# Additions of attention probabilities split by columns between VectorE and GpSimd, and ternary transposes at other steps

## The chip, the cores and the metric

The kernel runs on one core of a Trainium2 chip. The metric is the device time of one execution in microseconds. The engines in the tables: PE is TensorE (PEld its weight loads), DVE is VectorE, ACT is ScalarE, POOL is GpSimd, and SP issues nearly all DMAs.

## The reference

One transformer layer in float32: differential attention and a feed-forward layer with ternary weights, each behind a layer norm and with a residual. Shapes: 8 batches, 1024 rows, 512 columns, 16 heads of 32, hidden width 2048.

```python
qkv = x @ w_qkv                      # q, k split in halves of 16 columns per head: q1, q2, k1, k2
a1 = softmax(q1 @ k1.T * scale)
a2 = softmax(q2 @ k2.T * scale)
lam = exp(dot(lambda_q1, lambda_k1)) - exp(dot(lambda_q2, lambda_k2)) + 0.8
out = (a1 - lam * a2) @ v
out_n = out / rms(out) * norm_w * 0.2
x = x + rearranged(out_n) @ wo
# feed-forward
h = x @ (tern(w_fc) * scale).T + gate * (x @ v.T @ fast_b.T @ u.T)
x = x + relu(h) ** 2 @ (tern(w_proj) * scale).T
```

`tern(w)` is w over its row's mean magnitude, rounded and clipped to -1, 0, 1. What the change touches is the denominator of the softmax and the preparation of the ternary weights.

## The kernel before

The first phase (to about 130 us) loads and splits weights and projects the first batch. Then comes a loop over 64 pairs of heads, P = 0 to 63, eight for each batch (NP = 8). A pair has 16 steps, k = 0 to 15: j = k // 8 chooses the first or second softmax, t = k % 8 one of eight blocks of 128 key rows. The code counts in eight double steps d, with k = 2d and 2d + 1. The last phase (from about 2880 us) is the feed-forward layer.

In a step, PE multiplies keys by queries into PSUM (`pe_score`, L564, twice: c = 0 and 1 are the halves of the 1024 query rows); ACT takes the exponential of each half into one of four buffers of `pr` (`act_exp`, L921, 128x1024 each); PE multiplies them by v (`pe_pv`, L589); and the DVE adds them up into `acc[:, j]` (`dve_add`, L1222, 128x2048), which spares PE a sum per step. There is no addition at t = 0: that of t = 1 adds the first two blocks, so a pair has 14. Then PE multiplies `acc` by a matrix of ones (`pe_sum`, L610), for j = 0 at d = 5 of the same pair and for j = 1 at d = 1 of the next. ACT turns the sum into a reciprocal by logarithm and exponential (L927, L931).

In the last batch (P = 56 to 63, `pe_adds`) the DVE leaves out the addition of t = 7, and PE adds this block by four more matmuls (L618).

A buffer of `pr` is written again four steps later; `act_exp` waits for the product with v and, through `probabilities_read`, for the addition, or in the last batch for PE's sum. The semaphore `s_add` counts additions, `n_add` says how many are needed.

Every engine runs its own instruction list in order, and the order is written out by hand. Besides the steps, a pair carries:
- three projection tiles of the batch after (`pe_tile`, L503 and L506, in PSUM bank 6, cut into pieces by `PIECES`). ACT copies each (L900, L905), and the DVE subtracts the copy for the low part (`dve_low`, L1155) and takes a maximum (`dve_bound`, L1165). The next tile waits for L1155 (or for ACT's copy of a v tile).
- for a group of four pairs one layer norm of 512 rows of x: statistics, a short chain of 4-column operations (L1110 to L1116) and four normalisations (L1121), all on the DVE in the first two pairs, and PE's transposes (L479) in the others, from the second pair on.
- the work behind earlier pairs ("posts"): L1234 and L1237 combine the two softmaxes, PE transposes (L631), ACT copies (L946), GpSimd squares (`sq`, L283, 128x512, its only work in this loop), the DVE sums the squares (L1243), scales (L1248), splits (L1252), PE projects the output (L645, six matmuls each at d = 6 and 7), and the DVE adds the residual (L1258).
- in the last batch, with no projection left, one of eight 128-row pieces of the feed-forward weights per pair: magnitudes on ACT (L971), scales and comparisons on the DVE (L1280 to L1291, L1298), four groups of PE transposes (`pe_ternary`, L732) through PSUM bank 6, each copied by ACT (`act_ternary`, L982). The groups stand at d = 6 and 7 of the same pair, between the output projection and the last score of that double step, and at d = 0 and 1 of the next. The last two stand behind the loop.

Of the kernel before, what the change touches and what calls it, by code (L numbers as in the profile page):

```python
# [50 lines left out]
def probabilities_read(e, s_add, s_sum, f):  # L51

    P, j, t = f // 16, (f // 8) % 2, f % 8
    if t == 7 and pe_adds(P):
        e.wait_ge(s_sum, 2 * P + j + 1)
    else:
        e.wait_ge(s_add, n_add(P, j, t))
# [27 lines left out]
def build(nc, x, wqkv, wo, lq1, lq2, lk1, lk2, norm_w, fast_b, w_fc, w_proj, u, v, gate, out):  # L85
# [6 lines left out]
    with ExitStack() as top:  # L92
# [163 lines left out]
        def gpsimd_program(e):  # L256
# [12 lines left out]
            for X in range(NPAIR):  # L269
                if X == NPAIR - NP:  # L270

                    for r in range(2):
                        e.wait_ge(s_vsg[r], 16 * 2 * NC)
                    e.memset(fba[:], 0.0).then_inc(s_pool, 1)
                    e.memset(vrep[:], 0.0).then_inc(s_pool, 1)
                if X == NPAIR - 1:
                    e.wait_ge(s_sum, 2 * NPAIR)
                    e.memset(on1[:], 1.0).then_inc(s_pool, 1)

                e.wait_ge(s_raw, X + 1)  # L280
                if X:
                    e.wait_ge(s_ssq, X)
                e.tensor_tensor(sq[:], on[:], on[:], ALU.mult).then_inc(s_osq, 1)  # L283
# [309 lines left out]
        def pe_sum(e, X, j):  # L593
            e.wait_ge(s_add, n_add(X, j, 6 if pe_adds(X) else 7))
# [12 lines left out]
            for hh in range(2):  # L607
                for c in range(2):
                    c4 = 2 * hh + c
                    t = e.matmul(ps[32 * c4:32 * c4 + 32, bk, :], ones[:], acc[:, j, (2 * c + hh) * 512:(2 * c + hh + 1) * 512],  # L610
                                 start=True, stop=not pe_adds(X), skip_group_check=True)
            if pe_adds(X):
                gg = 16 * X + 8 * j + 7
                e.wait_ge(s_exp, n_half(gg, 1))
                for hh in range(2):
                    for c in range(2):
                        c4 = 2 * hh + c
                        t = e.matmul(ps[32 * c4:32 * c4 + 32, bk, :], ones[:], pr[:, gg % NPB, c, hh, :], start=False,  # L618
                                     stop=True, skip_group_check=True)
# [899 lines left out]
```

## Time and profile before

| What | us |
|---|---|
| Median of three runs | 3946.64 (3942.01 to 3947.13) |
| Profiled execution | 3940.3 |
| Its span, first to last instruction | 3938.6 |
| PE busy in the span | 3774.7 (96%) |
| DVE busy | 3205.4 (81%) |
| ACT busy | 2782.0 (71%) |
| POOL busy | 99.5 (3%) |
| DVE additions L1222, 880 of them | 1736.5 + 292.8 |

A profile comes from one execution. Busy time counts instructions running on an engine, and PE's is partly modelled, since matmuls are pipelined. A wait is idle time in front of an instruction, put down to what released it last. A row of a timeline gives start, duration, engine, line, operation and tiles; durations of neighbours on one engine overlap by some tens of nanoseconds, so starts tell the pace.

### The profile page before, as it was taken

The numbers are of one execution on the slowest core, as the hardware profiler recorded it, in microseconds if no ns is written. First come the engines' busy times: TensorE is split into PE (matmuls) and PEld (weight loads), VectorE is DVE, ScalarE is ACT, GpSimd is POOL, SyncE is SP. The second block draws the span as 40 slices with busy tenths as digits, with TensorE's granted clock in tenths as the row PEclk, the third lists the DMA queues.
The fourth block names the chain that finished last, engine by engine and source line by source line (L and its number), as shares of the span: only waits on it lengthen the run. The fifth ranks groups of instructions, "written<-read, shape, count | busy, mean of one in ns | idle before, by whom it ended". The sixth has DMA issues, their size and how long they took to land.

```text
span 3938.6 us, 57545 instructions
## 1 busy us (share of the span) xinstructions
PE 3774.7 (96%) x21960; PEld 2070.1 (53%) x21960; DVE 3205.4 (81%) x3089; ACT 2782.0 (71%) x3597; POOL 99.5 (3%) x78
## 2 busy tenths in 40 slices
PE   6799999999999999999999999999889999999999
PEld 5344444444444444444444444333378888888887
DVE  5699999999999999999999999988855555555554
ACT  2688888888888888888888888988733333333333
POOL 0000000000000000000000000000000000000000
PEclk9899999999999999999999999999989999999999
DMA  5545444445444445444444445433101010101010
GB/s 196 129 101 114 99 112 108 102 107 111 111 99 114 108 96 121 104 108 104 108 106 107 112 93 115 103 74 90 48 10 43 22 43 22 43 22 43 22 43 22
DMA packets 225844, 338.24 MB, mean 86 GB/s; under 512 B 86704, under 2 KB 107184, under 8 KB 225008
## 3 DMA queue, kind: packets, MB, share of 16 engines
q1 hardware_dynamic: 225520, 333.88, 34.7%
q8 instruction: 208, 3.41, 0.4%
q14 instruction: 116, 0.95, 0.1%
HBM read 180.72 MB, written 150.99 MB: 84 GB/s over the span
## 4 chain that ended last, share of the span: by engine, by line
PE 65%; DVE 22%; ACT 5%; issue 5%; DMA 1%; SPq 1%; DVEq 0%; ACTq 0%
DVE acc L1222 17%; PE ps L589 13%; PE ps L689 12%; PE ps L669 12%; PE ps L564 10%; PE ps L506 5%; PE ps L645 4%; PE ps L503 3%; ACT pr L921 3%; PE ps L610 2%; PE ps L674 1%; DVE stg L1155 1%; PE ps L719 1%; DVE ot L1234 1%; PE ps L709 1%
## 5 line engine op out<-in xcount | busy, mean ns | idle before, releaser
L921 ACT ACTIVATE pr<-ps 128x1024 f32<-128x1024 f32 x2048 | 1989.7, 1032 | 278.4 <-PE ps L564 272.3
L1222 DVE TENSOR_TENSOR acc<-acc,pr 128x2048 f32<-128x2048 f32 x752 | 1736.5, 2309 | 39.5 <-ACT pr L921 16.0
L589 PE MATMUL ps<-pr,vst 128*32 128x512 f32 x8192 | 1023.3, 601 | 0.0
L564 PE MATMUL ps<-qst,kst 50*128 50x512 f32 x4096 | 800.0, 460 | 58.9 <-ACT pr L921 38.0
L564 PEld LDWEIGHTS ps<-qst,kst 50*128 50x128 f32 x4096 | 339.3, 184 | 730.8 <-ACT pr L921 515.5
L1075 ACT ACTIVATE rb<-ps,scf 128x512 f32<-128x512 f32 x256 | 176.7, 690 | 388.4 <-PE ps L674 388.4
L589 PEld LDWEIGHTS ps<-pr,vst 128*32 128x32 f32 x8192 | 208.5, 109 | 429.2 <-issue 423.8
L689 PE MATMUL ps<-tP,hh_ 128*128 128x512 f32 x1024 | 404.4, 395 | 1.9 <-DVE hl_ L1442 1.9
L669 PE MATMUL ps<-yh,tT 128*128 128x512 f32 x1024 | 404.5, 395 | 0.0
L669 PE MATMUL ps<-yl,tT 128*128 128x512 f32 x1024 | 399.5, 390 | 0.0
L689 PE MATMUL ps<-tP,hl_ 128*128 128x512 f32 x1024 | 399.1, 390 | 0.0
L1440 DVE TENSOR_TENSOR sb<-rb 128x512 f32<-128x512 f32 x256 | 176.9, 691 | 268.7 <-ACT rb L1075 267.1
L1222 DVE TENSOR_TENSOR acc<-pr 128x2048 f32<-128x2048 f32 x128 | 292.8, 2288 | 110.4 <-ACT pr L921 109.0
L1442 DVE TENSOR_TENSOR hl_<-sb,hh_ 128x512 fp32r<-128x512 f32 x256 | 177.3, 693 | 179.3 <-ACT hh_ L1080 179.3
L1080 ACT ACTIVATE hh_<-sb 128x512 fp32r<-128x512 f32 x256 | 162.4, 635 | 205.3 <-DVE sb L1440 205.3
L503 PE MATMUL ps<-xth,wqh 128*128 128x512 f32 x512 | 222.1, 434 | 31.3 <-DVE stg L1155 31.3
L689 PEld LDWEIGHTS ps<-tP,hh_ 128*128 128x128 f32 x1024 | 192.1, 188 | 56.8 <-DVE fo L1480 12.6
L669 PEld LDWEIGHTS ps<-yl,tT 128*128 128x128 f32 x1024 | 192.5, 188 | 38.9
L669 PEld LDWEIGHTS ps<-yh,tT 128*128 128x128 f32 x1024 | 192.5, 188 | 38.5
L689 PEld LDWEIGHTS ps<-tP,hl_ 128*128 128x128 f32 x1024 | 192.3, 188 | 37.7
L503 PE MATMUL ps<-xtl,wqh 128*128 128x512 f32 x512 | 206.7, 404 | 0.0
L503 PE MATMUL ps<-xth,wql 128*128 128x512 f32 x512 | 202.3, 395 | 0.0
(154 smaller groups left out, 3493.6 us busy)
## 6 DMA issues: line engine op xcount, KB each, us to landing
qst<-q_scratch SPq DMA_DIRECT2D x128, 384.0 KB, 6.3
kst<-k_scratch SPq DMA_DIRECT2D x128, 384.0 KB, 9.6
q_scratch<-stg SPq DMA_DIRECT2D x168, 256.0 KB
k_scratch<-stg SPq DMA_DIRECT2D x168, 256.0 KB
xin<-in_L_attn_x_dram SPq DMA_DIRECT2D x16, 1024.0 KB, 5.4
v_scratch<-vsg SPq DMA_DIRECT2D x64, 256.0 KB, 3.1
vst<-v_scratch SPq DMA_DIRECT2D x128, 128.0 KB, 5.4
xr<-in_L_attn_x_dram SPq DMA_DIRECT2D x64, 256.0 KB
```

Source lines behind the costliest of these rows:

```text
L503: t = e.matmul(ps[:, bk, :], w[:, k, m0:m0 + 128], xx[:, k, :], start=(n == 0), stop=(n == 11))
L506: t = e.matmul(ps[:, bk, :], xx[:, k, st * 128:(st + 1) * 128], w[:, k, 2 * E:3 * E], start=(n == 0), stop=(n == 11))
L564: ins = e.matmul(ps[:, 2 * c + hh, :], kst[rows, r, j, t * 128:(t + 1) * 128], qst[rows, r, j, c * 512:(c + 1) * 512], start=True, stop=True)
L589: ins = e.matmul(ps[32 * c4:32 * c4 + 32, 4 + j, :], vst[:, r, t, 32 * hh:32 * hh + 32], pr[:, sl, c, hh, :], start=(t == 0), stop=(t == 7 ...
L669: e.matmul(ps[:, bk, :], tT[:, k, i * 128:(i + 1) * 128], y_[:, bf, k, :], start=(m == 0), stop=False)
L689: t = e.matmul(ps[:, rt, :], h_[:, uu % 3, rt * 128:(rt + 1) * 128], tP[:, i, :], start=(i == 0 and part == 0), stop=(i == 15 and part == 1))
L921: e.activation(pr[:, sl, c, :, :], ps[:, 2 * c:2 * c + 2, :], ACT.Exp, scale=SCALE).then_inc(s_exp, 1)
L1075: e.activation(rb[:, uu % 2, :], ps[:, 4 + uu % 2, :], ACT.Relu, scale=scf[:, 0, i:i + 1]) \
L1080: e.activation(hh_[:, uu % 3, :], sb2[:, uu % 2, :], ACT.Copy).then_inc(s_hh, 1)
L1222: e.tensor_tensor(acc[:, j, :], old, new, ALU.add).then_inc(s_add, 1)
L1440: e.tensor_tensor(sb2[:, uu % 2, :], rb[:, uu % 2, :], rb[:, uu % 2, :], ALU.mult).then_inc(s_sb, 1)
L1442: e.tensor_tensor(hl_[:, uu % 3, :], sb2[:, uu % 2, :], hh_[:, uu % 3, :], ALU.subtract) \
```

## The change

The additions are split by columns. GpSimd adds the first 512 of the 2048 columns (`GC`), which belong to the first exponential (c = 0), and waits for that one alone; the DVE adds the other 1536 and waits for the second exponential, as before. GpSimd counts in a semaphore of its own, `s_adg`, and whoever waited for `s_add` waits for both (`added`). GpSimd's squares, until now alone in its list, stand behind the addition of step 9 of the next pair.

In the last batch the addition of t = 7 is made as in all others, and PE's matmuls L618 are gone. The four groups of ternary transposes of a piece move to the double steps 0, 2, 3 and 4 of the next pair, where no output projection stands. ACT copies each behind the exponential of the odd step instead of in front of it. All four groups of the last piece now stand behind the loop.

```diff
+GC = 512
+TERNARY = (0, 2, 3, 4)
-def pe_adds(P):
-
-    return P >= NPAIR - NP
...
-    return (2 * P + j) * 7 - (2 * (P - NPAIR + NP) + j if pe_adds(P) else 0) + max(t, 1)
+    return (2 * P + j) * 7 + max(t, 1)
...
+        def added(e, P, j, t):
+
+            e.wait_ge(s_add, n_add(P, j, t))
+            e.wait_ge(s_adg, n_add(P, j, t))
...
+            for P in range(NPAIR):
+                for k in range(16):
+                    gpsimd_add(e, P, k)
+                    if k == 9:
...
+                        if P:
+                            gpsimd_square(e, P - 1)
...
+        def gpsimd_add(e, P, k):
+            gg, j, t = 16 * P + k, k // 8, k % 8
+            if t == 0:
+                return
+            e.wait_ge(s_exp, n_half(gg, 0))
+            new = pr[:, gg % NPB].rearrange("p c h n -> p (c h n)")[:, 0:GC]
+            if t == 1:
+                if P:
+                    e.wait_ge(s_sum, 2 * (P - 1) + j + 1)
+                else:
+                    e.wait_ge(s_wol, 1)
+                old = pr[:, (gg - 1) % NPB].rearrange("p c h n -> p (c h n)")[:, 0:GC]
+            else:
+                e.wait_ge(s_adg, n_add(P, j, t - 1))
+                old = acc[:, j, 0:GC]
+            e.tensor_tensor(acc[:, j, 0:GC], old, new, ALU.add).then_inc(s_adg, 1)
...
-                    if last and d >= 6:
-                        pe_ternary(e, P - (NPAIR - NP), d - 6)
-                    if last and d < 2 and P > NPAIR - NP:
-                        pe_ternary(e, P - (NPAIR - NP) - 1, d + 2)
+                    if P > NPAIR - NP and d in TERNARY:
+                        pe_ternary(e, P - (NPAIR - NP) - 1, TERNARY.index(d))
...
-                    if d >= 6 and tile >= 0:
-                        act_ternary(e, tile, d - 6)
-                    if d < 2 and tile >= 1:
-                        act_ternary(e, tile - 1, d + 2)
                     act_exp(e, P, k + 1, 1)
+                    if tile >= 1 and d in TERNARY:
+                        act_ternary(e, tile - 1, TERNARY.index(d))
...
-            e.tensor_tensor(acc[:, j, :], old, new, ALU.add).then_inc(s_add, 1)
+            e.tensor_tensor(acc[:, j, GC:], old, new, ALU.add).then_inc(s_add, 1)
```

How it moves instructions, at three places. First GpSimd's list, at the start of the loop before the change and its first three pairs behind it; the names in brackets are the semaphores waited for.

```order
14 L283 TENSOR_TENSOR sq<-on 128x512 [waits s_raw]
15 L283 TENSOR_TENSOR sq<-on 128x512 [waits s_ssq,s_raw] x55
16 L274 MEMSET fba 128x128 [waits s_vsg1,s_vsg0]
17 L275 MEMSET vrep 128x512
18 L283 TENSOR_TENSOR sq<-on 128x512 [waits s_ssq,s_raw] x7
```

```order
14 L296 TENSOR_TENSOR acc<-pr 128x512 [waits s_wol,s_exp]
15 L296 TENSOR_TENSOR acc<-acc,pr 128x512 [waits s_adg,s_exp] x6
16 L296 TENSOR_TENSOR acc<-pr 128x512 [waits s_wol,s_exp]
17 L296 TENSOR_TENSOR acc<-acc,pr 128x512 [waits s_adg,s_exp] x6
18 L296 TENSOR_TENSOR acc<-pr 128x512 [waits s_sum,s_exp]
19 L296 TENSOR_TENSOR acc<-acc,pr 128x512 [waits s_adg,s_exp] x6
20 L296 TENSOR_TENSOR acc<-pr 128x512 [waits s_sum,s_exp]
21 L302 TENSOR_TENSOR sq<-on 128x512 [waits s_ssq,s_raw]
```

From the second pair on, a pair has 14 additions on GpSimd and, behind the first one of the second softmax, one square; before it had the square alone.

Second, the DVE in the first pair of a group of four (with layer-norm statistics, L1099 before and L1108 after), from step 3 on.

```order
611 L1155 TENSOR_TENSOR stg<-ps,stg 128x512
612 L1099 BN_STATS st<-xin 128x6
613 L1222 TENSOR_TENSOR acc<-acc,pr 128x2048
614 L1099 BN_STATS st<-xin 128x6
615 L1222 TENSOR_TENSOR acc<-acc,pr 128x2048
616 L1165 TENSOR_REDUCE nmx<-stg 128x1
617 L1222 TENSOR_TENSOR acc<-acc,pr 128x2048
618 L1099 BN_STATS st<-xin 128x6
619 L1222 TENSOR_TENSOR acc<-acc,pr 128x2048
620 L1155 TENSOR_TENSOR stg<-ps,stg 128x512
621 L1222 TENSOR_TENSOR acc<-acc,pr 128x2048
```

```order
611 L1164 TENSOR_TENSOR stg<-ps,stg 128x512
612 L1108 BN_STATS st<-xin 128x6
613 L1230 TENSOR_TENSOR acc<-acc,pr 128x1536
614 L1108 BN_STATS st<-xin 128x6
615 L1230 TENSOR_TENSOR acc<-acc,pr 128x1536
616 L1174 TENSOR_REDUCE nmx<-stg 128x1
617 L1230 TENSOR_TENSOR acc<-acc,pr 128x1536
618 L1108 BN_STATS st<-xin 128x6
619 L1230 TENSOR_TENSOR acc<-acc,pr 128x1536
620 L1164 TENSOR_TENSOR stg<-ps,stg 128x512
621 L1230 TENSOR_TENSOR acc<-acc,pr 128x1536
```

Nothing moves on the DVE here; only the additions are shorter.

Third, ACT in the last batch, from double step 5 of P = 59 (rl are the reciprocals, ms and on belong to the posts, ta and scq to the magnitudes, tT receives the ternary transposes).

```order
1285 L927 ACTIVATE rl<-ps 128x512
1286 L931 ACTIVATE rl<-rl 128x512
1287 L921 ACTIVATE pr<-ps 128x1024 x6
1288 L949 ACTIVATE ms<-ms,small 128x16
1289 L953 ACTIVATE ms<-ms 128x16
1290 L982 ACTIVATE tT<-ps 128x4x128
1291 L921 ACTIVATE pr<-ps 128x1024 x4
1292 L982 ACTIVATE tT<-ps 128x4x128
1293 L921 ACTIVATE pr<-ps 128x1024 x2
```

```order
1291 L938 ACTIVATE rl<-ps 128x512
1292 L942 ACTIVATE rl<-rl 128x512
1293 L932 ACTIVATE pr<-ps 128x1024 x6
1294 L960 ACTIVATE ms<-ms,small 128x16
1295 L964 ACTIVATE ms<-ms 128x16
1296 L932 ACTIVATE pr<-ps 128x1024 x6
1297 L982 ACTIVATE ta,scq<-wf 128x512
1298 L932 ACTIVATE pr<-ps 128x1024 x2
1299 L969 ACTIVATE oth<-on 128x512
1300 L932 ACTIVATE pr<-ps 128x1024
1301 L993 ACTIVATE tT<-ps 128x4x128
```

The two copies of double steps 6 and 7 are gone from between the exponentials there; the next one comes behind the last exponential of double step 0 of the next pair.

## Rows read from the trace of the kernel before

**Rows 1.** Busy by stretch: us; then PE, PEld, DVE, ACT, POOL (count); clock, DMA.

```profile
300.00:2300.00 2000.00, 1955.17 (x12481) 868.26 (x12483) 1911.93 (x1460) 1721.91 (x2102) 74.53 (x47) 1.00 0.46 107
2503.00:2847.00 344.00, 311.30 (x2048) 110.02 (x2044) 299.57 (x271) 297.01 (x408) 8.92 (x10) 1.00 0.32 70
```

**Rows 2.** Waits, 200 to 2490 us: us in total, times, longest.

```profile
PE ps L503 <- DVE stg L1155: 30.5, 38, 1.7
...
PE ps L610 <- DVE xr L1258: 11.6, 12, 1.0
```

**Rows 3.** Timeline of PE: start, us, instruction, idle before and its releaser.

```profile
1507.41 0.50 PE L503 MATMUL ps<-xth,wqh 128*128 128x512 f32 x1 [1.66 <-DVE stg L1155]
```

**Rows 4.** Timeline of the DVE around 1505 us.

```profile
1504.48 2.27 DVE L1222 TENSOR_TENSOR acc<-acc,pr 128x2048 f32<-128x2048 f32 x1
1506.67 0.68 DVE L1155 TENSOR_TENSOR stg<-ps,stg 128x512 fp32r<-128x512 f32 x1
1507.27 2.53 DVE L1222 TENSOR_TENSOR acc<-acc,pr 128x2048 f32<-128x2048 f32 x1
```

**Rows 5.** Timeline of GpSimd: squares, one in a pair.

```profile
1505.57 2.08 POOL L283 TENSOR_TENSOR sq<-on 128x512 f32<-128x512 f32 x1 [38.95 <-ACT on L946]
1550.11 1.04 POOL L283 TENSOR_TENSOR sq<-on 128x512 f32<-128x512 f32 x1 [42.46 <-ACT on L946]
...
1674.40 2.08 POOL L283 TENSOR_TENSOR sq<-on 128x512 f32<-128x512 f32 x1 [39.01 <-ACT on L946]
...
2353.55 1.04 POOL L283 TENSOR_TENSOR sq<-on 128x512 f32<-128x512 f32 x1 [39.03 <-ACT on L946]
...
2477.31 2.23 POOL L283 TENSOR_TENSOR sq<-on 128x512 f32<-128x512 f32 x1 [40.35 <-ACT on L946]
...
2559.67 1.04 POOL L283 TENSOR_TENSOR sq<-on 128x512 f32<-128x512 f32 x1 [41.33 <-ACT on L946]
2602.64 1.04 POOL L283 TENSOR_TENSOR sq<-on 128x512 f32<-128x512 f32 x1 [41.92 <-ACT on L946]
```

**Rows 6.** Waits, 2490 to 2950 us.

```profile
ACT rl L927 <- PE ps L618: 20.2, 16, 4.7
...
ACT tP L982 <- PE ps L732: 12.0, 9, 1.8
ACT tT L982 <- PE ps L732: 11.2, 8, 1.8
```

**Rows 7.** Timeline of the DVE beside the square of 1550.11.

```profile
1550.59 2.71 DVE L1222 TENSOR_TENSOR acc<-acc,pr 128x2048 f32<-128x2048 f32 x1
```

**Rows 8.** Timeline of the DVE in the last batch, beside a square from 2645.62 to 2646.66.

```profile
2645.66 1.02 DVE L1287 TENSOR_SCALAR scf<-scf 128x4 f32<-128x4 f32 x1
2646.72 1.68 DVE L1291 TENSOR_SCALAR ta<-wf,scf 128x512 f32<-128x512 f32 x4
```

**Rows 9.** Timeline of the DVE: two additions with nothing between them.

```profile
1539.61 4.68 DVE L1222 TENSOR_TENSOR acc<-acc,pr 128x2048 f32<-128x2048 f32 x2
```

**Rows 10.** PE by line, 2503 to 2847 us: busy us, mean ns, idle before.

```profile
L618 PE MATMUL ps<-pr,ones 128*32 128x512 f32 x128 | 16.7, 592 | 0.0
```

**Rows 11.** Chain that ended last, 2656 to 2667 us: start, us, what.

```profile
2657.16 1.62 PE ps L645 x6
2658.78 0.45 PE ps L732 x4
...
2659.25 0.48 ACT tT L982
```

**Rows 12.** DVE by line, 2503 to 2847 us.

```profile
L1298 DVE SCALAR_TENSOR_TENSOR tt<-wf,scf,ta 128x512 f32<-128x512 f32 x16 | 11.3, 746 | 0.0
```

**Rows 13.** By line and shape, 300 to 2300 us.

```profile
L1222 DVE TENSOR_TENSOR acc<-acc,pr 128x2048 f32<-128x2048 f32 x566 | 1308.6, 2312 | 26.9 <-ACT pr L921 11.6 <-DVE acc L1222 1.0
...
L1222 DVE TENSOR_TENSOR acc<-pr 128x2048 f32<-128x2048 f32 x95 | 217.3, 2287 | 49.5 <-ACT pr L921 48.3
...
L1237 DVE TENSOR_TENSOR ot<-ot,rl 128x512 f32<-128x512 f32 x48 | 33.2, 692 | 1.7
```

More of the change, by code:

```diff
@@ L38, in n_half @@
     return 2 * gg + c + 1
-def pe_adds(P):
-    return P >= NPAIR - NP
 def n_add(P, j, t):
-    return (2 * P + j) * 7 - (2 * (P - NPAIR + NP) + j if pe_adds(P) else 0) + max(t, 1)
[L51 to L57, printed above, removed]
+    return (2 * P + j) * 7 + max(t, 1)
 def sum_bank(P, j):
@@ L212, in build @@
             sem(n) for n in ("s_xt", "s_xth", "s_xtl", "s_tile", "s_qh", "s_ql", "s_qx", "s_v", "s_flv", "s_flp"))
-        s_sc, s_exp, s_add, s_pv, s_gpe, s_gdve = (
-            sem(n) for n in ("s_sc", "s_exp", "s_add", "s_pv", "s_gpe", "s_gdve"))
+        s_sc, s_exp, s_add, s_adg, s_pv, s_gpe, s_gdve = (
+            sem(n) for n in ("s_sc", "s_exp", "s_add", "s_adg", "s_pv", "s_gpe", "s_gdve"))
         s_sum, s_rln, s_rex, s_pt, s_ot, s_tr, s_raw, s_osq, s_ssq, s_rmln, s_rmex, s_on, s_oth, s_otl, s_owo, s_x2v = (
@@ L268, in gpsimd_program, with gpsimd_square @@
                             channel_multiplier=-1).then_inc(s_pool, 1)
[L269 to L283, printed above, removed]
+            for P in range(NPAIR):
+                for k in range(16):
+                    gpsimd_add(e, P, k)
+                    if k == 9:
+                        if P == NPAIR - NP:
+                            for r in range(2):
+                                e.wait_ge(s_vsg[r], 16 * 2 * NC)
+                            e.memset(fba[:], 0.0).then_inc(s_pool, 1)
+                            e.memset(vrep[:], 0.0).then_inc(s_pool, 1)
+                        if P:
+                            gpsimd_square(e, P - 1)
+            e.wait_ge(s_sum, 2 * NPAIR)
+            e.memset(on1[:], 1.0).then_inc(s_pool, 1)
+            gpsimd_square(e, NPAIR - 1)
+        def gpsimd_add(e, P, k):
[14 more added lines that the diff above has]
+            e.tensor_tensor(acc[:, j, 0:GC], old, new, ALU.add).then_inc(s_adg, 1)
+        def gpsimd_square(e, X):
+            e.wait_ge(s_raw, X + 1)
+            if X:
+                e.wait_ge(s_ssq, X)
+            e.tensor_tensor(sq[:], on[:], on[:], ALU.mult).then_inc(s_osq, 1)
         def sync_x(e, C):
@@ L593, in pe_sum @@
         def pe_sum(e, X, j):
-            e.wait_ge(s_add, n_add(X, j, 6 if pe_adds(X) else 7))
+            added(e, X, j, 7)
             bk = sum_bank(X, j)
@@ L610, in pe_sum @@
                     t = e.matmul(ps[32 * c4:32 * c4 + 32, bk, :], ones[:], acc[:, j, (2 * c + hh) * 512:(2 * c + hh + 1) * 512],
[L611 to L619, printed above, removed]
+                                 start=True, stop=True, skip_group_check=True)
             t.then_inc(s_sum, 1)
@@ L837, in tensor_program @@
             pe_pv(e, NSLOT - 3)
+            pe_ternary(e, 7, 0)
             pe_pv(e, NSLOT - 2)
+            pe_ternary(e, 7, 1)
+            pe_pv(e, NSLOT - 1)
             pe_ternary(e, 7, 2)
-            pe_pv(e, NSLOT - 1)
             pe_ternary(e, 7, 3)
@@ L914, in act_exp @@
                     e.wait_ge(s_pv, f + 1)
-                    probabilities_read(e, s_add, s_sum, f)
+                    added(e, f // 16, (f // 8) % 2, f % 8)
                 else:
@@ L1043, in scalar_program @@
                     act_posts(e, P, d, 1)
-                    if d >= 6 and tile >= 0:
-                        act_ternary(e, tile, d - 6)
-                    if d < 2 and tile >= 1:
-                        act_ternary(e, tile - 1, d + 2)
                     act_exp(e, P, k + 1, 1)
+                    if tile >= 1 and d in TERNARY:
+                        act_ternary(e, tile - 1, TERNARY.index(d))
             act_post(e, NPAIR - 2, 8, 1)
-            act_ternary(e, 7, 2)
-            act_ternary(e, 7, 3)
+            for m in range(4):
+                act_ternary(e, 7, m)
             act_post(e, NPAIR - 1, 1, 0)
@@ L1207, in dve_add @@
             gg, j, t = 16 * P + k, k // 8, k % 8
-            if t == 0 or (t == 7 and pe_adds(P)):
+            if t == 0:
                 return
-            sl = gg % NPB
             e.wait_ge(s_exp, n_half(gg, 1))
-            new = pr[:, sl].rearrange("p c h n -> p (c h n)")
+            new = pr[:, gg % NPB].rearrange("p c h n -> p (c h n)")[:, GC:]
             if t == 1:
```

6 lines of the change are left out of this document (3 added, 3 removed).

## The prediction

> **What bounds the kernel now.** I read the views in this order: busy time by stretch, waits by engine, the timelines of the DVE, PE and GpSimd, and the chain.
>
> The stretch from 300 to 2300 us stands for the pair loop of batches 0 to 6. PE is busy 1955 of 2000 us there and the DVE 1912; ACT has room with 1722, GpSimd nearly everything [rows 1]. PE is the bound and the DVE stands close behind it. What PE loses to the DVE is in the waits of 200 to 2490 us: 30.5 us before a projection matmul, for the subtraction that frees its bank, and 11.6 us before the matmuls of a sum [rows 2]. One such wait: PE stood still for 1.66 us until L1155 was done [rows 3], and L1155 stood in the DVE's queue behind an addition that ran from 1504.48 to 1506.75 [rows 4]. So the additions' length reaches PE through the queue.
>
> The squares at L283 come once in a pair of heads and mark its period [rows 5]. From 1505.57 to 1674.40 four pairs take 168.8 us, 42.2 each; the first takes 44.5. From 2353.55 to 2477.31 three pairs without layer-norm steps and without transposes of x take 41.25 each. Four of those are 165.0, so a group of four has 3.8 us on top. About 2 us of it are PE's own transposes of x, the rest is waiting.
>
> In the last batch (2503 to 2847) a pair takes 43.0 us (2559.67 to 2602.64) [rows 5]. PE is busy only 311 of 344 us, the DVE 300, ACT 297 [rows 1]. The chain alternates between PE and ACT, and ACT waits 20.2 us for the sums and 12.0 + 11.2 us for the ternary transposes [rows 6].
>
> **The addition split by columns.** The DVE keeps 1536 of 2048 columns. A 2048-column addition takes 2.27 us and a 512-column operation 0.68 [rows 4], so 512 columns are worth 0.53 us and the DVE's part takes 1.74. At 14 additions a pair that frees 7.4 us of the DVE's queue. GpSimd has the same operation on 512 columns in the trace: 1.04 us [rows 5], 15.6 us a pair with the square, of 42: as an engine it is no bound.
>
> The cost lies where the two meet. At 1505.57 GpSimd's square started under a running addition and took 2.08 us instead of 1.04: it ended at 1507.65, 0.90 after the addition's end at 1506.75. The next addition started at 1507.27, took 2.53 us, and ended at 1509.80, 2.15 after the square [rows 4, 5]. At 1550.59 an addition that started 0.48 us into a square took 2.71 [rows 7]. L1155, which reads PSUM and one SBUF tile, took its usual 0.68 us beside the waiting square [rows 4]. A DVE operation with two SBUF inputs and a GpSimd tensor operation exclude each other here. Even a 4-column scalar operation of the DVE, L1287, took 1.02 us beside a square [rows 8], so in the last batch the ternary comparisons count as excluded too.
>
> The Trainium skill, SBUF — State Buffer, section "Who interferes with whom", has this as an exclusive lock held for a whole instruction, taken by a DVE operation with two SBUF inputs and by a GpSimd operation that reads SBUF; the trace agrees (0.90 and 2.15 us behind each other's ends). Were there no lock, the whole 7.4 us would leave the DVE's queue and this part would come out at its lower bound.
>
> So an addition now costs 0.90 for GpSimd and 2.15 - 0.53 = 1.62 for the DVE, 2.52 us in a row. What pays is what else stands between two additions on the DVE, since an operation with at most one SBUF input fits beside GpSimd's 0.90. Starts lie 2.19 us apart behind an addition and 0.60 behind a 512-column operation [rows 4]; two additions in a row start 2.39 apart (4.68 - 2.29) [rows 9]. By what stands between two additions, before and after:
> - nothing: 2.39 to 2.52, +0.13;
> - one operation that reads PSUM or one tile: 2.79 to 2.52, -0.27;
> - two of them: 3.39 to 1.62 + 1.20 = 2.82, -0.57;
> - one with two SBUF inputs: 2.79 to about 3.06, +0.27;
> - one of each: 3.39 to 3.06, -0.33.
>
> Counted along the DVE's order, a mean pair has 3.5, 5.75, 1.0, 1.25 and 1.5 of these, and one that is mixed. That gives 0.46 - 1.55 - 0.57 + 0.34 - 0.50 = -1.8 us a pair. I give back 0.8 for collisions off this pattern: a GpSimd addition that takes the lock just ahead of L1248, L1252, L1121 or a tiny layer-norm step costs up to 0.90, and there are 4 to 7 of these in a pair. Net the DVE's queue is 1 us a pair shorter, of 40.4 (1912 / 2000 x 42.2).
>
> What does PE get of that? I walked the lock through the stretch of [rows 4] with the exponentials at their recorded times, starting at the pair's first addition. The addition that ended at 1506.75 ends at 1505.6, L1155 1.1 us earlier than 1507.35, and the wait of 1.66 shrinks to 0.5. In the second half of the same pair, with the layer-norm steps, the addition before the sum ends only 0.2 us earlier, since two collisions eat the lead. In the pairs without layer norm there is hardly a wait to remove. All waits named are 42 us [rows 2]; I take two thirds, **-28 us**. Bounds: -46 (all of them and 4 more of the same kind), and above nothing, by the second rival.
>
> GpSimd now also holds the square behind its own addition at step 9 of a pair; its reader on the DVE stands two steps of 2.6 us later, so this costs nothing as long as GpSimd is within two steps. New waits: ACT's exponentials, PE's sums and SP's first two loads of x2 wait for both counters. ACT waits for an addition four steps back, so GpSimd may lag 10 us before ACT stands, with PE's scores behind it.
>
> **The last batch.** PE loses the 16 groups at L618 (16.7 us busy [rows 10]), most of them on the chain ahead of the logarithm. The ternary transposes leave the steps with the output projection: there the chain ran 1.62 us of projection, 0.45 of transpose and 0.48 of copy before the next exponential [rows 11]. Now the exponential follows the projection, twice in a pair: 0.9 x 2. The copies still cost ACT the same elsewhere. PE and ACT could so gain 0.9 x 2 + 0.9 x 2 = 3.6 us a pair at best, 29 in eight.
>
> But the DVE gets two more additions a pair. Its lock chain: 14 x 2.52 = 35.3, the square 0.9, three operations with two SBUF inputs 1.8, four of L1298 at 0.66 = 2.6 [rows 12], four of L1291 at 0.40 = 1.6 [rows 8], tiny ones 0.6: 42.8 us, with all PSUM readers hidden. That is the 43.0 of today. I take **0** for the batch, between -20 (half hidden behind ACT's own work) and +12 (1.5 a pair of collisions). At the end two more ternary transposes stand behind the last exponential, some 2 x 0.45 on PE and a copy, +2, against 0.9 for the last L618 group: +1, which I count with the zero.
>
> Sum: -28 on the profiled execution (3940.3 around a span of 3938.6) and the same on the median: 3946.6 - 28 = **3919 us**, with 3900 to 3935 as this case's own range.
>
> **Rivals.** *More than that*: all waits on the DVE go and the last batch follows PE and ACT, -46 - 20: about 3881. For it speaks that 7.4 us a pair leave the DVE; against it the lock chain of 42.8. Chance 0.08.
>
> *No change*: the lock gives back what the shorter addition frees. Two collisions of 0.9 us a pair in place of one are enough. Then the DVE's queue is as long as before, about 3946. The Trainium skill, Perfetto Trace Analysis, section "Optimizing Scalar/DVE Operations", warns that moving work between GpSimd and DVE "might not help" because of the shared port. The trace bears it out for additions with nothing between them, and there are 3.5 in a pair. Chance 0.17.
>
> *Slower*: GpSimd's 0.90 isn't hidden. GpSimd's addition is ready one exponential ahead of the DVE's; it can find the lock free while the DVE waits or works on PSUM, and still hold it when the DVE's addition comes. Unhidden, a pair pays 14 x 0.90 = 12.6 against 7.4, +5.2 on 40.4: 45.6 against a period of 42.2, +3.4 x 56 + 2 x 8 = +206. It decides when less than about 3.4 of the 5.5 us of non-excluded work a pair run beside GpSimd (DVE work besides additions is (1912 - 1526) / 47.4 = 8.1, of it four operations a pair like L1237, an estimated 2.6, excluded [rows 1, 13]). At half hidden it is +0.6 a pair and +12 in the last batch, +46 or about 3993, and at a third +100. Chance 0.27.
>
> **How the numbers follow.** Forecast 0.48, more 0.08, none 0.17, slower 0.27. Within 0.2% is 3938.7 to 3954.5, about what a measurement of this kernel can tell from no change. Faster 0.56, same 0.17, slower 0.27. For 8 in 10 the range runs from 3880 (the larger gain) to 3995, which leaves out the worse part of the slower case.
>
> **What would show it.** Steps right: the DVE's addition at a median near 1.75 us but a mean of 2.1 or more, since it waits for the lock; GpSimd's addition spread from 1.04 to 2.7; PE's wait before projections down from 30.5 us to 10 or so; the first pair of a group nearer 42.5 than 44.5. Wrong: GpSimd additions at 1.04 beside running DVE additions (no lock: then -46 in the first part), PE or ACT waiting for GpSimd's addition, or PE's wait for L1155 grown. In the last batch the period tells: 43.0 if the lock chain holds it, 40 if not.

## The result, and the profile after

The kernel with the change takes **4044.4 us** (median of four runs, 4044.1 to 4045.1) against 3944.3 for the kernel before beside it: ratio 1.0254, interval 1.0236 to 1.0272. It is 100 us slower, where 28 us less were forecast. The profiled execution has a span of 4042.8 us.

Busy time by stretch, with the columns of [rows 1]. The second stretch holds most of the last batch, whose pairs now take 47.3 us instead of 42.7 to 43.0.

```profile
300.00:2300.00 2000.00, 1916.99 (x12140) 845.75 (x12136) 1894.65 (x1428) 1675.60 (x2044) 1384.16 (x689) 0.99 0.45 105
2565.00:2930.00 365.00, 304.04 (x1842) 101.61 (x1842) 353.18 (x269) 296.57 (x400) 230.24 (x118) 0.93 0.28 63
```

In the first stretch PE did less work (12140 matmuls against 12481, 1917 us against 1955), and its granted clock was 0.99 instead of 1.00. In the last batch the DVE is busy 353 of 365 us.

Waits of PE from 200 to 2490 us, which answer [rows 2], and then two from 2565 to 2930 us.

```profile
PE ps L522 <- DVE stg L1164: 40.5, 63, 1.0
PE ps L629 <- DVE xr L1266: 36.9, 25, 2.4
```

```profile
PE ps L629 <- DVE xr L1266: 14.2, 7, 3.1
ACT pr L932 <- DVE acc L1230: 14.2, 16, 1.7
```

PE's wait before a projection for the subtraction of the low part (L522; L503 in the kernel before) grew from 30.5 to 40.5 us. Its wait before a sum for the addition of the residual (L629; there L610) grew from 11.6 to 36.9, and the longest of these from 1.0 to 2.4. Now the groups by line and shape of the DVE and GpSimd, 300 to 2300 us, which answer [rows 13].

```profile
L1230 DVE TENSOR_TENSOR acc<-acc,pr 128x1536 f32<-128x1536 f32 x552 | 1190.1, 2156 | 33.5 <-ACT pr L932 19.3 <-DVE acc L1230 1.0
L296 POOL TENSOR_TENSOR acc<-acc,pr 128x512 f32<-128x512 f32 x551 | 1155.4, 2097 | 392.7 <-ACT pr L932 365.0
L1230 DVE TENSOR_TENSOR acc<-pr 128x1536 f32<-128x1536 f32 x92 | 188.3, 2046 | 39.2 <-ACT pr L932 39.2
...
L1260 DVE TENSOR_TENSOR otl<-on,oth 128x512 fp32r<-128x512 f32 x46 | 81.7, 1777 | 0.0
L1256 DVE TENSOR_TENSOR on<-on,ms 128x512 f32<-128x512 f32 x46 | 68.3, 1485 | 0.0
...
L1119 DVE TENSOR_TENSOR ln_t<-rs 128x4 f32<-128x4 f32 x12 | 14.8, 1234 | 0.0
L1125 DVE SCALAR_TENSOR_TENSOR rs<-ln_t,rs 128x4 f32<-128x4 f32 x12 | 13.7, 1145 | 0.4
```

An undisturbed addition of 1536 columns takes 1.75 us; the mean is 2.16. In 46 pairs the additions wait (1190.1 + 188.3 - 644 x 1.75) / 46 = 5.5 us a pair. The split of the output (L1260; there L1252) takes 1.78 us, undisturbed 0.68; the scaling (L1256) 1.49, undisturbed 0.68; two of the layer norm's 4-column operations (L1119, L1125) 1.2 instead of 0.16. These, with L1130 and L1180, make another 2.9 us a pair. The shorter additions save 14 x 0.53 = 7.4. The DVE waits 8.4.

How long GpSimd holds is in the timelines. First two additions of the DVE, then GpSimd's between them.

```profile
1531.40 1.74 DVE L1230 TENSOR_TENSOR acc<-acc,pr 128x1536 f32<-128x1536 f32 x1
1533.06 0.68 DVE L1108 BATCH_NORM_STATS2 st<-xin 128x6 f32<-128x512 f32 x1
1533.66 2.23 DVE L1230 TENSOR_TENSOR acc<-acc,pr 128x1536 f32<-128x1536 f32 x1
```

```profile
1532.27 2.01 POOL L296 TENSOR_TENSOR acc<-acc,pr 128x512 f32<-128x512 f32 x1 [0.86 <-ACT pr L932]
```

GpSimd's addition ends at 1534.28, **1.14 us** after the DVE's (1533.14); in 749 cases, all in which GpSimd's addition starts under a running one of the DVE and ends behind it, the middle four fifths lie between 1.136 and 1.151. The DVE's next one ends 1.61 behind it. The forecast had 0.90 and 1.62.

**Where the time sits.** The first exponential of each pair marks the periods. By place in a group of four pairs, batches 0 to 6 without the first four pairs, and in the last batch:

| us a pair | first | second | third | fourth | last batch |
|---|---|---|---|---|---|
| before | 42.85 | 43.45 | 41.57 | 41.27 | 42.73 |
| after | 43.23 | 46.57 | 42.64 | 41.29 | 47.27 |

There are 13 such groups: +0.4, +3.1, +1.1 and 0 give +60 us, of it 41 in the second pairs. With the first four pairs, batches 0 to 6 are 61 us longer (2426.7 against 2365.8), and the last batch gives 8 x 4.5 = +36. Behind the last exponential come 7 more (1106.7 against 1099.9). That makes the 104 us between the two profiled executions. Here is a second pair, 1560.4 to 1607.3: PE's timeline, PE's clock by stretch, and the DVE's and GpSimd's timelines ahead of the wait.

```profile
1564.56 1.06 PE L608 MATMUL ps<-pr,vst 128*32 128x512 f32 x8
1568.03 1.93 PE L629 MATMUL ps<-acc,ones 128*32 128x512 f32 x8 [2.40 <-DVE xr L1266]
1569.71 1.89 PE L608 MATMUL ps<-pr,vst 128*32 128x512 f32 x8
```

```profile
1565.60:1568.00 2.40, 0.03 (x4) 0.00 (x1) 2.40 (x3) 0.90 (x1) 1.43 (x1) 0.99 1.04 164
1568.00:1572.00 4.00, 3.97 (x20) 0.97 (x20) 3.44 (x4) 1.23 (x2) 0.34 (x1) 0.58 0.54 95
1572.00:1607.00 35.00, 33.99 (x218) 15.87 (x218) 32.84 (x25) 30.04 (x37) 22.87 (x13) 1.00 0.30 88
```

```profile
1560.22 1.51 DVE L1130 TENSOR_SCALAR xin<-xin,mv,rs 128x512 f32<-128x512 f32 x1
1561.66 1.75 DVE L1230 TENSOR_TENSOR acc<-acc,pr 128x1536 f32<-128x1536 f32 x1
1563.33 0.68 DVE L1256 TENSOR_TENSOR on<-on,ms 128x512 f32<-128x512 f32 x1
1563.93 0.54 DVE L1130 TENSOR_SCALAR xin<-xin,mv,rs 128x512 f32<-128x512 f32 x1
1564.38 2.84 DVE L1230 TENSOR_TENSOR acc<-acc,pr 128x1536 f32<-128x1536 f32 x1
1567.14 0.74 DVE L1266 SCALAR_TENSOR_TENSOR xr<-ps,nw,xr 128x512 f32<-128x512 f32 x1
```

```profile
1564.15 1.45 POOL L296 TENSOR_TENSOR acc<-pr 128x512 f32<-128x512 f32 x1 [2.70 <-ACT pr L932]
```

GpSimd got ahead of the addition of 1564.38, which so took 2.84 us; the residual L1266 stood behind it, and PE behind the residual for 2.40 us. In the kernel before the same wait is 0.95 us:

```profile
1531.93 1.06 PE L610 MATMUL ps<-acc,ones 128*32 128x512 f32 x8 [0.95 <-DVE xr L1258]
```

And after this wait the granted clock is 0.58 for 4 us, near the lower level of 1.2 GHz: eight sum matmuls take 1.93 us, where the same eight took 1.06 before, and the next group 1.89, where it took 1.06 at 1564.56. That is 1.45 us of wait and 1.7 of clock, 3.1 of the pair. From 300 to 2300 us there are 12 second pairs, and 12 such waits of 2.38 to 2.41; the clock fell at each.

### The profile page after: what moved, and what is told of

The parts are those of the page before. It is cut to its first block, busy times and chain, and to the rows that moved or that the text cites. A ratio compares the mean times of both kernels' runs of the same rounds, so it can differ in the third digit from the quotient of the medians.

```text
span 4042.8 us, 60260 instructions
## 1 busy us (share of the span) xinstructions
PE 3799.8 (94%) x21832; PEld 2070.9 (51%) x21832; DVE 3317.1 (82%) x3105; ACT 2788.5 (69%) x3597; POOL 1942.2 (48%) x974
## 3 DMA queue, kind: packets, MB, share of 16 engines
q14 instruction: 139, 1.14, 0.1%
## 4 chain that ended last, share of the span: by engine, by line
PE 57%; DVE 28%; issue 8%; ACT 4%; SPq 1%; DMA 1%; DVEq 0%; POOL 0%; ACTq 0%
DVE acc L1230 22%; PE ps L700 12%; PE ps L680 12%; PE ps L608 10%; PE ps L583 7%; PE ps L525 4%; PE ps L522 3%; PE ps L629 3%; PE ps L656 2%; ACT pr L932 2%; DVE stg L1164 1%; PE ps L685 1%; ACT rl L942 1%; ACT rl L938 1%; DVE tt L1306 1%
## 5 line engine op out<-in xcount | busy, mean ns | idle before, releaser
L296 POOL TENSOR_TENSOR acc<-acc,pr 128x512 f32<-128x512 f32 x768 | 1621.7, 2112 | 537.5 <-ACT pr L932 496.6
L1230 DVE TENSOR_TENSOR acc<-acc,pr 128x1536 f32<-128x1536 f32 x768 | 1667.8, 2172 | 47.6 <-ACT pr L932 24.0
L608 PE MATMUL ps<-pr,vst 128*32 128x512 f32 x8192 | 1041.1, 610 | 0.0
L296 POOL TENSOR_TENSOR acc<-pr 128x512 f32<-128x512 f32 x128 | 232.6, 1817 | 456.1 <-ACT pr L932 456.1
L1230 DVE TENSOR_TENSOR acc<-pr 128x1536 f32<-128x1536 f32 x128 | 261.6, 2044 | 76.1 <-ACT pr L932 76.0
L522 PE MATMUL ps<-xth,wqh 128*128 128x512 f32 x512 | 221.9, 433 | 40.9 <-DVE stg L1164 40.5
```

The source lines that it names most:

```text
L296: e.tensor_tensor(acc[:, j, 0:GC], old, new, ALU.add).then_inc(s_adg, 1)
L522: t = e.matmul(ps[:, bk, :], w[:, k, m0:m0 + 128], xx[:, k, :], start=(n == 0), stop=(n == 11))
L608: ins = e.matmul(ps[32 * c4:32 * c4 + 32, 4 + j, :], vst[:, r, t, 32 * hh:32 * hh + 32], pr[:, sl, c, hh, :], start=(t == 0), stop=(t == 7 ...
L1230: e.tensor_tensor(acc[:, j, GC:], old, new, ALU.add).then_inc(s_add, 1)
```

## The experiments

The line of the DVE's additions is L1273 in e2, e9, e11 and e12 and L1272 in e7, e8 and e10; in e2, e9, e11 and e12 scaling and split are L1299 and L1303. In all of these a function `splits(P, k)` names the steps whose addition is split; the others stay whole on the DVE. Each ratio is against the kernel before run beside it.

**The parts apart.** e1: the kernel before with the ternary transposes moved alone.

```diff
-                    if last and d >= 6:
-                        pe_ternary(e, P - (NPAIR - NP), d - 6)
-                    if last and d < 2 and P > NPAIR - NP:
-                        pe_ternary(e, P - (NPAIR - NP) - 1, d + 2)
+                    if P > NPAIR - NP and d in TERNARY:
+                        pe_ternary(e, P - (NPAIR - NP) - 1, TERNARY.index(d))
```

> The kernel before with the second part of the change alone: the ternary transposes at the double steps 0, 2, 3 and 4 of the next pair, PE's extra sum matmuls kept, no split. Theory L (the lock between GpSimd and DVE makes the loss) expects no loss here: today's last batch waits on PE and ACT in turn, so leaving the projection steps frees up to 1.8 us a pair; 3930 to 3945. Rival T (the moved transposes are to blame for the last batch, whose pairs went from 43.0 to 47.3 us) expects 47 us pairs and some 3975.

Measured: 3937.97 us, ratio 0.9993 (0.9983 to 1.0002). The difference can't be told from none.

e3: as e1, and the addition of t = 7 on the DVE in the last batch too; the change without its split.

```diff
 def pe_adds(P):
-    return P >= NPAIR - NP
+    return False
```

> The changed kernel without the split: all 14 additions whole on the DVE in all pairs, PE's extra sum matmuls gone, transposes moved. Theory L expects the DVE at about 35.6 + 4.4 = 40 us a pair of the last batch, under the 43.0 of before, so a gain or no change against before: 3925 to 3950. If the additions of t = 7 on the DVE made the loss of the last batch, it shows 45 us pairs and +16 or more.

Measured: 3944.3 us, 1.0009 (0.9996 to 1.0022), 42.5 us a pair in the last batch. What the change does beside the split costs at most 9 us. Behind the last exponential this kernel takes 1104.0 us against 1099.9, so about 4 of the 7 us that the change loses there come without the split.

e2: the kernel before with the split in batches 0 to 6 alone.

```diff
+def splits(P, k):
+    return k % 8 > 0 and P < NPAIR - NP
```

> The column split alone, in batches 0 to 6; the last batch as before in all respects. Theory L expects the loss of the pair loop, +4.6 us a group of four pairs as between the two profiles (169.1 to 173.7), 13 groups: +60, about 4005. Rival T expects nearly all of the loss to be gone, within 15 us of before.

Measured: 4003.75 us, 1.0158 (1.0141 to 1.0175), with the pairs of the table to within 0.02 us and 42.86 in the last batch. The split costs 63 us in the first seven batches; the full change costs 37 more (100 against 63, each over the kernel before run beside it), with what it does in the last batch.

**The lock.** e4: the full change, GpSimd's addition replaced by a memset of the same columns with the same waits. It leaves out the sum of the first 512 columns.

```diff
-            e.tensor_tensor(acc[:, j, 0:GC], old, new, ALU.add).then_inc(s_adg, 1)
+            e.memset(acc[:, j, 0:GC], 1.0).then_inc(s_adg, 1)
```

> The changed kernel with GpSimd's addition replaced by a memset of the same 512 columns, so the sum of these columns is left out; all waits and counters stay. It reads no SBUF. Theory L expects no stretch of the DVE's additions (1.75 us each) and the whole 7.4 us a pair off the DVE's queue: faster than before, 3870 to 3910. Rival W (the new waits on GpSimd's counter and the later start of its work cost the time, whatever it does) expects most of the loss to stay, 4000 or more.

Measured: 3871.12 us, 0.982 (0.9803 to 0.9836). By line and shape, 300 to 2300 us, and the busy time of that stretch:

```profile
L1230 DVE TENSOR_TENSOR acc<-acc,pr 128x1536 f32<-128x1536 f32 x582 | 1020.7, 1754 | 113.2 <-ACT pr L932 106.9
L296 POOL MEMSET acc<- 128x512 f32 x680 | 359.3, 528 | 1594.3 <-ACT pr L932 1594.3
```

```profile
sum 2000.00, PE 2000.00 PEld 895.23 DVE 1606.37 ACT 1770.19 POOL 408.52; mean PE 2000.00 PEld 895.23 DVE 1606.37 ACT 1770.19 POOL 408.52
```

With every semaphore and wait of the change in place but nothing read by GpSimd, the additions take 1.75 us and PE never stands. So the new waits by themselves cost nothing. Batches 0 to 6 are 60 us faster than in the kernel before (2306.1 against 2365.8; the forecast's bound for a DVE without a lock was 46) and the last batch 12. The 173 us between this kernel and the changed one come with GpSimd's addition in place of the memset. The memset is also the shorter of the two (0.53 us against 1.27), which this run alone does not set apart from the reads; e5 changes the reads. The Trainium skill, SBUF — State Buffer, section "Who interferes with whom", says that a DVE instruction with two SBUF inputs contends with a GpSimd instruction that reads SBUF and not with one that only writes it; the trace agrees, 0.53 us for the memset and 1.75 for the addition beside it.

e5: the full change, GpSimd's addition reads one tile twice. The sum of those columns isn't the reference's.

```diff
-            e.tensor_tensor(acc[:, j, 0:GC], old, new, ALU.add).then_inc(s_adg, 1)
+            e.tensor_tensor(acc[:, j, 0:GC], new, new, ALU.add).then_inc(s_adg, 1)
```

> The changed kernel with both inputs of GpSimd's addition the same 512 columns of pr, so the sum of these columns is not the sum of the blocks. Theory L, with the hold taken from the operands: a GpSimd operation that reads one place twice, like the square, ends 0.90 us after the DVE's addition, one that reads two places 1.14. Then the hold falls to 0.90 here, and the kernel comes to where the forecast stood, 3915 to 3960. Rival A (the hold of 1.14 belongs to the addition, or to the wait on its own counter, not to the operands): hold 1.14 and some 4044 again.

Measured: 3963.09 us, 1.0044 (1.0028 to 1.0061). GpSimd's operation alone, and the DVE's mean:

```profile
1503.78 1.04 POOL L296 TENSOR_TENSOR acc<-pr 128x512 f32<-128x512 f32 x1 [1.49 <-ACT pr L932]
```

```profile
L1230 DVE TENSOR_TENSOR acc<-acc,pr 128x1536 f32<-128x1536 f32 x565 | 1100.8, 1948 | 61.6 <-ACT pr L932 53.2 <-DVE acc L1230 0.5
```

It takes 1.04 us alone and holds 0.90 (median of 675 cases), just as the square did. The hold follows the tiles read: 0.90 for one tile twice, 1.14 for two. The quarter microsecond costs 81 us in the whole kernel (4044.4 - 3963.1). But with the forecast's own 0.90 this one is still 21 us slower than before. Its second pairs take 45.04 us and its last batch 44.51 a pair. One of those second pairs: PE's wait, and the stretch behind it.

```profile
1542.82 0.50 PE L522 MATMUL ps<-xth,wqh 128*128 128x512 f32 x1 [1.94 <-DVE stg L1164]
```

```profile
1542.80:1546.80 4.00, 3.98 (x14) 2.99 (x16) 3.90 (x2) 0.28 (x1) 2.53 (x1) 0.65 0.36 90
```

Again one wait of 1.94 us and then a clock of 0.65. From 300 to 2300 us there are 12 such waits, and the clock fell at 9 of them. In the kernel before the longest, 1.66 us [rows 3], comes in each group of four too. The mean clock of 1.00 [rows 1] hides that it fell there as well, but only at 4 of the 12. Here are the 4 us behind the wait that ended at 491.88:

```profile
491.90:495.90 4.00, 4.00 (x18) 1.86 (x22) 3.79 (x4) 1.36 (x3) 0.22 (x1) 0.64 0.35 87
```

e6: the full change with 256 columns.

```diff
-GC = 512
+GC = 256
```

> The changed kernel with GC = 256 in place of 512. Theory L: between 128x512 and 128x256 GpSimd's hold falls from 1.14 to some 0.6 us and the DVE's part is 1.88, so with nothing between two additions they start 2.5 us apart instead of 2.76 (2.39 unsplit), and with one operation hidden 2.5 against 2.79 unsplit. That is 2 us a pair less on the DVE than before: 3915 to 3945. Rival F (the hold is a fixed cost of any GpSimd instruction): hold stays near 1.1, the DVE frees only 0.27 an addition, and the time is over 4044, about 4080.

Measured: 3944.7 us, 1.0000 (0.9989 to 1.0012). GpSimd holds 0.59 us (675 cases), the DVE's 1792 columns end 1.88 behind it: 2.47 in a row. Second pairs take 43.53, the last batch 44.16 a pair. The ratio of 1.0000 is a sum of two: batches 0 to 6 are 13 us shorter than in the kernel before (2352.6), the last batch 11 us longer and what stands behind it 5.

**Which collisions.** e9: as e2, but whole where operations that GpSimd's turn would hold up stand beside the addition: steps 3 and 15 (scaling and split of the output) in every pair, 13 and 14 in the first pair and 1 in the second pair of a group (layer norm).

```diff
 def splits(P, k):
-    return k % 8 > 0 and P < NPAIR - NP
+    return P < NPAIR - NP and k % 8 > 0 and k not in (3, 15) + ((13, 14), (1,), (), ())[P % 4]
```

> The split of 512 columns in batches 0 to 6 alone, as in the run that had 4004, but not at the steps where the DVE has an operation with two SBUF inputs or a layer-norm step ahead of its addition (steps 3 and 15; 13 and 14 in the first pair of a group of four, 1 in the second). Theory C: beside the longer hold, what the forecast missed is that GpSimd's addition gets in front of each of these operations (L1260 took 1.78 us instead of 0.69 in every pair), worst where the layer-norm steps stand, so the second pair of a group comes down from 46.6 us to 44.5 or less and the time to 3965 to 3985. Without theory C only the number of split steps counts: 2.9 of 14 fewer a pair, a fifth of the loss of 62, so about 3991.

Measured: 3925.78 us, 0.9964 (0.995 to 0.9978). Leaving 2.75 of 14 additions whole moved the time by 78 us, 39 below the lower end of what I had expected; the second pairs fell from 46.55 to 42.49. Two more kernels tell the two kinds of collision apart. e11 leaves out the layer norm's steps alone, e12 steps 3 and 15 alone.

```diff
+    return P < NPAIR - NP and k % 8 > 0 and k not in ((13, 14), (1,), (), ())[P % 4]
```

> The additions split at 512 columns in batches 0 to 6 and the last batch as before (4003.75 us), but left whole at three of the steps where the layer norm's short operations stand beside them: 13 and 14 in the first pair of a group of four, 1 in the second; 0.75 of 14 a pair. GpSimd so takes no lock ahead of the 4-column operations and of the first normalisations. If the loss sits in these places, above all in the second pair (46.55 us a pair), most of the way to the kernel that leaves out steps 3 and 15 as well (3925.8) is gained here: 3930 to 3950, with the second pair near 43. If it sits in the output's scaling and split, two operations a pair with two SBUF inputs at steps 3 and 15, little changes here: 3985 to 4000.

```diff
+    return P < NPAIR - NP and k % 8 > 0 and k not in (3, 15)
```

> As the split in batches 0 to 6 (4003.75 us), but left whole at steps 3 and 15 of every pair, where the scaling (128x512, two SBUF inputs) and the split of the output stand beside them; 2 of 14 a pair. If the loss sits there: 3930 to 3950. If it sits in the layer norm's operations: the second pair stays near 46 and the time is 3975 to 4000. If the two add up: about 1.1 us a pair of additions waiting saved for each operation of 1.1 freed, 3950 to 3975 here.

Measured: e11 3994.02 us, 1.0138 (1.0121 to 1.0155); e12 3939.31, 0.9997 (0.9988 to 1.0007). So 10 us come from the layer norm's steps and 64 from the output's; together 74 of the 78. By the number of splits alone e12 would have gained 2 of 14 parts of 63, 9 us. The output's two operations by line, in e2 and then in e12, 300 to 2300 us:

```profile
L1303 DVE TENSOR_TENSOR otl<-on,oth 128x512 fp32r<-128x512 f32 x46 | 81.7, 1776 | 0.0
L1299 DVE TENSOR_TENSOR on<-on,ms 128x512 f32<-128x512 f32 x46 | 68.3, 1484 | 0.0
```

```profile
L1299 DVE TENSOR_TENSOR on<-on,ms 128x512 f32<-128x512 f32 x47 | 44.9, 956 | 0.0
...
L1303 DVE TENSOR_TENSOR otl<-on,oth 128x512 fp32r<-128x512 f32 x48 | 32.8, 683 | 0.0
```

That is 1.6 us a pair. The second pair gained 3.0 by it, and its clock shows why more came back than was taken away. One second pair of e11, then one of e12:

```profile
1553.60:1600.00 46.40, 43.42 (x274) 19.62 (x268) 42.78 (x33) 37.00 (x47) 27.35 (x15) 0.96 0.43 103
```

```profile
1524.60:1568.30 43.70, 41.82 (x274) 18.80 (x268) 42.60 (x35) 36.82 (x46) 30.20 (x13) 1.00 0.47 110
```

PE does the same work in 43.4 us at a clock of 0.96 and in 41.8 at 1.00. In e11 the layer norm's steps are free and the sum's wait is down to 0.36 us, but one of 2.62 stands before a projection instead, behind an L1303 of 1.75 us; in this pair of e12 the longest is 1.26. Of waits over 1.4 us there are 12 in e2, of 2.40 to 2.42, and the clock fell at all 12; 12 in e11, of 2.62 to 2.64, and it fell at 9; none in e12 and e9, where from 300 to 2300 us it never fell. At 1.7 us each the 12 falls of e2 are 20 of e12's 64 us.

**A version that gains.** e8 and e7 split only where one or two operations that don't collide stand behind the addition, in batches 0 to 6, with 512 and with 256 columns, and move the ternary transposes.

```diff
+def splits(P, k):
+    return P < NPAIR - NP and (k in (1, 2, 5, 7, 9, 10, 11, 12) or k in ((4, 6) if P % 4 == 0 else (13,)))
```

> As the run with selected steps and 256 columns, with 512 columns. Theory L: hold 1.14 beside one hidden operation of 0.60 gives 2.76 against 2.79, no gain; beside two of them 2.82 against 3.39. About 0.7 us a pair off the DVE in sum: 3925 to 3945, that is behind the 256 columns though twice the work leaves the DVE. If the number of columns taken off the DVE decided, it would be the faster of the two.

> Before with the transposes moved and 256 columns split off, but only in batches 0 to 6 and only at steps where an operation with at most one SBUF input stands ahead of the DVE's addition. Theory L: every hold of 0.6 us is hidden behind such an operation of 0.60, 8 to 9 in a pair at -0.27: 2.3 us off the DVE, without the cost elsewhere; the first two pairs of a group lose some 1.3 us each: 3900 to 3920. Rival F: 0.5 us unhidden at each, no gain, 3945 to 3980.

Measured: e8 3915.01 us, 0.9919 (0.9899 to 0.9938); e7 **3897.56**, 0.9877 (0.9857 to 0.9896). It is 44 us below the kernel before beside it and 147 below the changed one. Both came out below what I had expected, e8 by 10 us and e7 by 2. From 300 to 2300 us the clock falls in neither, where it fell four times in the kernel before; the expectations had no term for that. The stretch of e7 from 300 to 2300 us, and its wait for the projection's low part:

```profile
sum 2000.00, PE 1986.00 PEld 886.05 DVE 1851.07 ACT 1756.33 POOL 765.70; mean PE 1986.00 PEld 886.05 DVE 1851.07 ACT 1756.33 POOL 765.70
```

```profile
PE ps L550 <- DVE stg L1203: 10.3, 12, 0.9
```

PE is busy 1986 of 2000 us, and that wait is 10.3 us instead of 30.5.

e10: as e7, and in the last batch t = 7 on the DVE, with a split at steps 1, 2, 10 and 11.

> The version with 256 columns at selected steps, carried into the last batch: split there too at the steps 1, 2, 10 and 11, and the additions of t = 7 on the DVE in place of PE's matmuls. Theory L: the DVE's load in the last batch is about 40 us a pair less 4 x 0.27, under the 42.5 that the batch takes, and PE gives up 1.8 us a pair: 41.5 a pair, 3888 to 3897. If ACT sets the pace there, 42.5 a pair stay and the time is that of the version before, 3898.

Measured: 3898.28 us, 0.9891 (0.9874 to 0.9907). The last batch takes 42.09 us a pair, e7's 42.52, and the kernel gains nothing by it: the 3.5 us gained there come back behind the last exponential, where e10 takes 1104.0 us and e7 1100.7. What sets the last batch's pace then was not looked into further.

## Why the prediction was wrong

**What bounds the kernel** was right, and so was the mechanism: PE in front, the DVE's queue close behind, and a lock between DVE operations with two SBUF inputs and GpSimd's. e4 shows it from the other side. What failed are sizes in the sum, four of them, and a price that the sum did not have.

**GpSimd's hold, 0.90, was the first step that failed.** I took it from the square, which reads one tile twice. The addition reads two: 1.14. The DVE's half, 1.62, was exact. With 1.14 the forecast's own table changes sign: two additions in a row cost 2.76 instead of 2.52; "nothing between" is +0.37, one harmless operation -0.03, two still -0.57, one with two SBUF inputs +0.51, one of each -0.09. With the same counts that is 1.30 - 0.17 - 0.57 + 0.64 - 0.14 = +1.1 a pair for the DVE instead of -1.8, before any collision. e5 prices the step at 81 us.

**The collisions, 0.8 a pair, were the second.** Of the 4 to 7 places in a pair it counted about one as a full collision. In fact L1256, L1260, L1130 and the layer norm's small operations waited 2.9 us a pair. (The two corrections can't be added up: at 43.4 us a pair, 1894.65 us busy of 2000 are 41.1 a pair, against 40.4 before: the queue grew by 0.7 and not by 1.1 + 2.9, so they show which way the terms were wrong and not the exact size. The forecast had -1.) GpSimd's addition is ready one exponential ahead of the DVE's, so it takes the lock as soon as an addition of the DVE ends, and whatever follows there with two SBUF inputs waits 1.1 us, in each of 46 cases at L1260 (mean 1.78 against 0.68). The "slower" rival named this. e11 and e12 show that the two output operations carry most of it (64 of 78 us), and the layer norm little, though it stands in the pairs that lost most.

**What PE gets, -28, was the third,** since it was read as a share of the waits that vanish. With the forecast's hold (e5) batches 0 to 6 are 13 x (-1.42 + 1.59 + 0.18 - 0.01) = +4 us. The first pair gained 1.4, near what the walk through the lock had. The second pair, where the walk did not go, lost 1.6, and there a wait grew long enough for the clock to fall behind it in 9 of 12 cases. No term of the sum had a price for TensorE's clock: 1.7 us each time, 12 times in the change and 4 in the kernel before from 300 to 2300 us, so some 14 us of the 61.

**The last batch, 0 between -20 and +12,** was +36. The lock chain of 42.8 us is with a hold of 1.14: 14 x 2.76 + 0.9 + 1.8 + 2.6 + 1.6 + 0.6 = 46.1, where 47.3 was measured; the comparisons L1306 cost 1.4 to 1.6 us each instead of 0.75 [rows 12]. The sum's main term was too small. With 0.90 (e5) it is 44.5 against 42.8. At the end the forecast had +1, and 7 were measured. In this batch the clock fell too, to a mean of 0.93 against 1.00 before; since the DVE is busy 353 of 365 us, part of that may be hidden behind it, and no run tells how much. The ternary move did not give the 3.6 us a pair that it could at best (e1: -3 us in eight pairs, within what can be told).

**No new waits**: right. GpSimd's lag cost PE and ACT nothing in e4, and in the change's own trace none of their waits ends at GpSimd. In the last batch ACT waited 14.2 us for additions of the DVE, not of GpSimd.

**The rivals.** "Slower" was the case, at its worse part: 3993 at half hidden and 4047 at a third (3946.6 + 100). That 4047 lies so near the 4044 measured is luck: it used 0.90 as well, had no clock in it, and even unhidden allowed the last batch only 2 x 8 = 16 us, where 36 were measured. With 0.27 I gave it too little; the range was cut just where it begins. The Trainium skill's warning, in Perfetto Trace Analysis, section "Optimizing Scalar/DVE Operations", that such a move "might not help", was held for no change; here it is a loss of 2.5% with 512 columns at every step, nothing with 256 (e6), and a gain of 1.2% with 256 at chosen steps (e7).

## What to carry to other kernels

Take the time that one engine holds another from an operation with the same operands: a square of one tile was 0.90 us, a sum of two 1.14, and a table of 14 such terms a pair turned from -1.8 to +1.1. Before work goes from the DVE to GpSimd, mark each DVE operation with two SBUF inputs behind the place, and split only where others stand there (e12 against e2: 64 us for two places of 14). Let the piece be small (256 columns against 512: 100 us at every step, e6 against the change, and 17 at chosen steps, e7 against e8). And when the DVE's delay lands on a TensorE that is the bound, look at the longest single wait beside the sum of waits: it may cost once more in the clock.

## What the runs showed of the hardware

- GpSimd's operation ends behind the end of the DVE operation that held it up by 1.14 us (512 columns, two tiles), 0.90 (512, one tile read twice), 0.59 (256, two tiles). Alone the same take 1.27 to 1.31, 1.04 and 0.73.
- A GpSimd memset of 512 columns took 0.53 us and held up nothing.
- A DVE operation on 4 columns waits as long as one on 1536: L1119 took 1.23 us instead of 0.16. L1130, which reads one tile of 512 columns and two columns of scalars from SBUF, was held up too: 1.51 us instead of 0.54.
- The granted clock fell to 0.58 over the 4 us behind a PE wait of 2.40 us (0.65 behind one of 1.94), and the same eight matmuls took 1.93 us instead of 1.06. From 300 to 2300 us it fell at 12 of 12 waits of 2.4 us (the change), at 9 of 12 of 2.63 (e11), 9 of 12 of 1.94 (e5) and 4 of 12 of 1.66 (the kernel before), and at none of the waits up to 1.39 in e8, e9 and e12. In the last batch of the change it also fell during a wait of 1.32 us, and was 0.50 behind it:

```profile
2687.92 0.79 PE L583 MATMUL ps<-qst,kst 50*128 50x512 f32 x2 [1.32 <-ACT pr L932]
```

```profile
2690.00:2694.00 4.00, 4.00 (x14) 2.33 (x10) 4.00 (x4) 0.53 (x2) 2.09 (x2) 0.50 0.14 39
```

So a long wait makes the fall likelier, but its length alone does not decide. What else does is left open.

- The same kernel differs from one execution to the next with the clock. Of 19 executions of the kernel before, beside e1 to e4, the shortest took 3935.89 us at a mean clock of 0.993, the longest 3952.28 at 0.989.
